# A fused two-layer transformer kernel on one core: first norms and weights reordered, two key batches closed in three steps, filler products on TensorE

## The reference

```python
x = L0_attn_hidden_states                       # (2, 1024, 256)
xn = _layernorm(x)
x = x + _L0_attn_ref(xn, ...) + _L0_ffn_ref(xn, ...)
xn = _layernorm(x)
x = x + _L1_attn_ref(xn, ...) + _L1_ffn_ref(xn, ...)

def _L0_attn_ref(h, ...):     # linear attention, 16 heads of 16
    qp, kp = elu(q) + 1.0, elu(k) + 1.0
    kv = einsum('bhsd,bhse->bhde', kp, v)
    z = einsum('bhsd,bhd->bhs', qp, kp.sum(axis=2))[..., None]
    return (einsum('bhsd,bhde->bhse', qp, kv) / (z + EPS)) @ o_w.T + o_b

def _L0_ffn_ref(x, ...):      # weights cut to -1, 0, 1 times mean(|W|)
    return (silu(x @ wu.T) * (x @ wg.T)) @ wd.T

def _L1_attn_ref(x, ...):     # rotary positions, softmax(q k / 4) v
def _L1_ffn_ref(x, ...):      # Hadamard transforms around a silu-gated FFN
```

## Time and profile before

| | before |
|---|---|
| median of 3 runs | 740.97 us (739.71, 740.97, 741.88) |
| the profiled execution's own time | 741.94 us |
| its span, first to last instruction | 740.0 us |
| mean granted TensorE clock | 0.975 |
| PE busy | 696.3 us, 94% |
| DVE / ACT / POOL busy | 71% / 59% / 40% |

### The profile page before, as it was taken

How to read it: one execution, slowest core, us unless ns; L and a number is a source line. 1 busy time by engine, 2 the same in 40 slices (tenths; PEclk the granted TensorE clock), 3 DMA queues, 4 the chain that set the end, 5 groups by cost and what they waited for, 6 DMA issues and landing times.

```text
span 740.0 us, 10943 instructions
## 1 busy us (share of the span) xinstructions
PE 696.3 (94%) x4186; PEld 437.3 (59%) x4186; DVE 524.2 (71%) x856; ACT 438.6 (59%) x600; POOL 295.8 (40%) x269
## 2 busy tenths in 40 slices
PE   3788899989999899999999998999999999999998
PEld 3576798977787778677677673333333333333345
DVE  4877866555578366678788878888897288888315
ACT  2454334446544532432432336999998899999883
POOL 1118846347657843542543431122224223333410
PEclk7799999999999999999999998999999999999999
DMA  6127101003024553423110112244444244423321
GB/s 260 57 77 279 58 0 58 1 2 115 0 86 152 182 166 98 140 90 115 57 58 2 57 58 76 80 144 151 139 138 149 93 147 141 157 90 94 102 81 58
DMA packets 25847, 74.13 MB, mean 100 GB/s; under 512 B 4620, under 2 KB 5996, under 8 KB 24964
## 3 DMA queue, kind: packets, MB, share of 16 engines
q1 hardware_dynamic: 21268, 65.37, 26.4%
q0 software_dynamic: 3808, 7.60, 3.5%
q10 hardware_dynamic: 720, 0.48, 0.2%
HBM read 54.54 MB, written 23.06 MB: 105 GB/s over the span
## 4 chain that ended last, share of the span: by engine, by line
PE 62%; POOL 2%; DVE 2%; ACT 1%; issue 1%; DMA 1%; SPq 0%; DVEq 0%; POOLq 0%; ACTq 0%
PE PS L1029 17%; PE PS L767 12%; PE PS L1015 12%; PE PS L773 9%; PE PS L998 6%; PE PS L988 5%; DVE mx L1329 1%; POOL sg L1642 1%; ACT P L1541 1%; DMA scr_k<-spl 1%; POOL rot L1663 1%; POOL rot L1662 1%; PE PS L1004 0%; ACT spl L1523 0%; ACT us L1506 0%
## 5 line engine op out<-in xcount | busy, mean ns | idle before, releaser
L1541 ACT ACTIVATE P<-PS 128x1024 f32<-128x1024 f32 x256 | 249.2, 1023 | 31.9 <-PE PS L1015 31.6
L1336 DVE TENSOR_REDUCE mx<-PS 128x1 f32<-128x512 f32 x300 | 189.2, 683 | 34.3 <-PE PS L998 32.7
L1329 DVE TENSOR_REDUCE mx<-PS 128x2 f32<-128x1024 f32 x106 | 124.8, 1221 | 37.4 <-PE PS L988 37.0
L1029 PE MATMUL PS<-P,VV 128*32 128x512 f32 x1024 | 137.6, 609 | 0.1
L1633 POOL TENSOR_TENSOR hl<-sg,hh 128x512 fp32r<-128x512 f32 x64 | 85.2, 1332 | 116.7 <-ACT hh L1511 67.4
L1015 PEld LDWEIGHTS PS<-QS,KS 64*128 64x128 f32 x512 | 48.9, 185 | 124.3 <-ACT P L1541 111.2
L1015 PE MATMUL PS<-QS,KS 64*128 64x512 f32 x512 | 117.7, 459 | 2.3 <-DVE mx L1329 1.8
L998 PE MATMUL PS<-KM,QM 64*128 64x512 f32 x300 | 82.0, 401 | 0.0
L1497 ACT ACTIVATE sg<-PS,cols 128x512 f32<-128x512 f32 x32 | 22.0, 688 | 82.1 <-PE PS L767 82.1
L1642 POOL TENSOR_TENSOR sg<-sg,us 128x512 f32<-128x512 f32 x32 | 42.1, 1316 | 37.5 <-ACT us L1506 37.5
L767 PE MATMUL PS<-XH,UGH 128*128 128x512 f32 x128 | 54.2, 423 | 1.6 <-ACT sg L1497 0.8
(11 more groups left out here) (211 smaller groups left out, 1346.6 us busy)
## 6 DMA issues: line engine op xcount, KB each, us to landing
QM<-scr_q SPq DMA_DIRECT2D x16, 512.0 KB, 4.4
KM<-scr_k SPq DMA_DIRECT2D x16, 512.0 KB, 5.3
QS<-scr_q SPq DMA_DIRECT2D x16, 512.0 KB, 4.3
KS<-scr_k SPq DMA_DIRECT2D x16, 512.0 KB, 5.2
scr_q<-spl SPq DMA_DIRECT2D x24, 256.0 KB, 3.3
scr_k<-spl SPq DMA_DIRECT2D x24, 256.0 KB, 3.4
scr_o<-OE POOLq DMA_DIRECT2D x14, 256.0 KB, 2.7
stg<-in_tern SPq DMA_DIRECT2D x3, 1024.0 KB, 4.8
```

The costliest lines, as they stand in the source:

```text
L1029: i = e.matmul(PS[32 * c:32 * c + 32, 7, :], v_head(8 * b + kt, 2 * j + c // 2), P[s % 4][:, chunk(c // 2 + 2 * (c % 2))], start=(kt == 0) ...
L1329: e.tensor_reduce(mx[p % 2][:, :, qt, half], PS[:, b:b + 2, :], AX.X, ALU.max).then_inc(q["mx"], 2)
L1336: e.tensor_reduce(mx[p % 2][:, h, qt, half:half + 1], bank[b], AX.X, ALU.max).then_inc(q["mx"], 1)
L1541: e.activation(P[s % 4][:, half * 1024:(half + 1) * 1024], PS[:, b:b + 2, :].rearrange("p b n -> p (b n)"), ACT.Exp).then_inc(q["ex"], 1)
```

## The change

- The first pieces are reordered: norm 1 ahead of turn 0, stats 2 and turn 0 ahead of the first weights; stats 3, norm 3 and turn 3 later among the first key tiles; the four POOL bias additions one to three pieces earlier.
- `FIRST` goes from 12 to 11 and `RATE0` from 0.8 to 0.83, so the FFN of layer 0 begins one side step earlier and the side work is advanced a little faster.
- `kv_end` yields after the last `kv_sum`, and again after the last three `kv_out`, so FFN pieces come between them. The two `kv_end` together have four steps more than before.
- Filler products (`busy`): 20 instead of 8 at `start`; 6 and 6 into bank 7 ahead of the first key tile, the second six after W0H; 5 into bank 2 ahead of `att_n(3)`; 4 and 2 ahead of the first and second score step. Their results are never read.

```diff
--- before.py
+++ after.py
@@ -17,10 +17,10 @@
 EARLY, MOST = 106, 3
 
 PROJECT = (56, 112, 120)
-FIRST = 12
+FIRST = 11
 
 WHOLE = 2
-RATE0 = 0.8
+RATE0 = 0.83
 
 COST = {"v": 0.7, "ln_turn": 1.0, **{n + a: 0.7 for n in ("gate", "up", "down") for a in ("", "_a")}}
 APART = 2.06
@@ -57,6 +57,9 @@
         self.i = (self.i + 1) % len(self.slots)
         return self.slots[self.i]
 
+    def peek(self):
+        return self.slots[(self.i + 1) % len(self.slots)]
+
     def pair(self):
         if self.i % 2 == 0:
             self.next()
@@ -114,8 +117,10 @@
 
     def kv_end(b):
         put("kv_sum", 8 * b + 7)
+        yield
         for tt in range(8 * b + 5, 8 * b + 8):
             put("kv_out", tt)
+        yield
         put("kv_sums", b)
         yield
 
@@ -124,6 +129,8 @@
         yield
 
     def att_n(tt):
+        if tt == 3:
+            put("busy", 5, 2)
         put("att_n", tt, ps.next())
         yield
 
@@ -279,30 +286,27 @@
     put("start")
     put("load_wa0")
     ln0 = [layernorm(c, pf) for c in range(NCH)]
-    for i in (0, 1, 0):
+    for i in (0, 1, 0, 1, 0, 2):
         next(ln0[i])
     put("w0h")
-    for i in (0, 1):
-        next(ln0[i])
     put("w0l")
-    for i in (1, 2):
-        next(ln0[i])
+    next(ln0[1])
+    put("busy", 6, 7)
+    put("busy", 6, 7, "w0h", 1)
+    next(tn)
     put("signs")
     sd0 = side0()
     next(sd0)
     next(ln0[2])
-    next(tn)
     next(sd0)
-    next(ln0[2])
-    next(ln0[3])
     for n in range(FIRST):
         if n < 10:
             next(tn)
         next(sd0)
-        if n < 2:
-            next(ln0[3])
-        if n > 7:
-            put("bias", 0, n - 8)
+        if n < 4:
+            next(ln0[2 if n == 0 else 3])
+        if n > 6:
+            put("bias", 0, n - 7)
     put("half")
     put("load_down")
     put("load_ob1")
@@ -408,6 +412,8 @@
                         later(PROJECT[g] + i, "project", g, i // 2, i % 2)
             elif piece[0] in ("times", "high", "low", "join"):
                 put(*piece)
+        if s < 2:
+            put("busy", 4 - 2 * s, mxr.peek())
         if live:
             put("scores", s, 0, st.pair())
             for _ in range(kept):
@@ -785,7 +791,14 @@
 
             def start():
                 e.wait_ge(q["init"], 1)
-                sums(bank[7][:, 0:128], [(ONES[:, :], ONES[:, :])] * 8)
+                sums(bank[7][:, 0:128], [(ONES[:, :], ONES[:, :])] * 20)
+
+            def busy(n, b, *after):
+
+                claim(b)
+                if after:
+                    e.wait_ge(q[after[0]], after[1])
+                sums(bank[b][:, 0:128], [(ONES[:, :], ONES[:, :])] * n)
 
             def ln_turn(n, *banks):
                 for b in banks:
@@ -1083,7 +1096,7 @@
                             o = two_tiles(bank[acc[2 * cc + i]], r, ((LH[:, ts], WLH[:, cc, :]), (LH[:, ts], WLL[:, cc, :]), (LL[:, ts], WLH[:, cc, :])), False, True)
                         o.then_inc(q["lp"], 1)
 
-            parts = {f.__name__: f for f in (start, ln_turn, tern_scale, kv_in, kv_out, q0, att_n, att_t, att_b, add_vb, prep_down, prep_ug,
+            parts = {f.__name__: f for f in (start, busy, ln_turn, tern_scale, kv_in, kv_out, q0, att_n, att_t, att_b, add_vb, prep_down, prep_ug,
                                              gate_a, gate, up_a, up, down_a, down, ffn_end, qk, v, max_half, max_rows, scores, values, project, last)}
             parts["max"] = max_tile
             for name, *args in order:
```

## The result

| | before | after |
|---|---|---|
| median of 4 runs each | 740.91 us (739.71 to 741.88) | **747.41 us** (746.14 to 747.69) |
| ratio, 95% interval | | **1.0086** [1.0074, 1.0098] |
| profiled execution, its span | 741.94, 740.0 | 747.69, 745.6 |

The forecast was 737.8, faster; the kernel became 6.5 us slower, and lies outside the range. In the diff's lines those of the helpers moved by 6 (L767 is L773), the ones of DVE, ACT and POOL by 13 (L1419 is L1432).

What follows compares the result with a forecast made beforehand. PE, busy 94% of the span, bounds the kernel; gains come only from its idle or half-clock time. 741.94 - 1.1 (first part) - 3.0 (first scores) = 737.8 us, range 733.0 to 742.5.

Steps and rivals of the forecast that it cites:

- The middle: 80 to 445 us: the same pieces shift by a place or two; 0 gained, with 1.5 us either way.
- The start: First norms, weights and key tiles: first key product at 18.8 us, 1.1 us earlier; first two tiles 2.5 us less.
- What eats it: First FFN blocks: PE waits of 2.8, 2.3 and 5.6 us reduce the 3.8 us lead to 1.1.
- that of 5.6 us: First FFN chunk: PE idle 5.6 us ahead of the first `down`, until DVE's second cut of TD at 70.9.
- my 1.1: Net gain of the first part: 2.6 - 3.2 + 2.85 - 1.1 = 1.1 us.
- my 3.2 us of deferred work: Tile 9, `att_n(2)` and `att_b(0)`, done before the first `down` in the kernel before, now come later: -3.2 us.
- the lead stays: Rival: DVE fills its waits, PE waits about 2 us at the first `down`; first part +5, total 733.9; chance 0.22.
- The fillers ahead of attention result 3: Five fillers ahead of `att_n(3)`, 10 records at 0.113: cost 1.1 us, since PE is no longer idle there.
- The first scores: Fillers there are hidden and keep the clock from falling at 448.2: 3.0 us gained, or 0 if it falls.
- The slower rival: TD's cuts come no earlier, PE's idle at the first `down` brings half clock: first part -4.7, total 743.6; chance 0.12.
- The base of the sum: The sum starts from the profiled execution, 741.94 us; the median of the runs shown was 740.97.
- my 0.8 us: If GpSimd and DVE exclude each other, `kv_sum(3)` beside a bias addition stands 0.8 us, total 738.6; nothing was added.

Runs made afterwards that it cites:

- the start alone: Kernel before with the new order of norms and weights and the start fillers; FIRST, RATE0 and kv_end as before, no other fillers: 735.47 us (0.9915).
- the fastest one: Kernel before with the changed start (norms, weights, start fillers) and the fillers at the first scores, the rest as before: 733.94 us (0.9888).
- both rows: Changed kernel with norm 7 ahead of the split of tile (1, 0), and that tile's join ahead of layer 0's last FFN end: 740.34 us (1.0001).
- the raised tail: Changed kernel with 0.08 more side steps per FFN step from step 72 of layer 0's FFN on: 743.02 us (1.0027).

## Why the prediction was wrong

- **The middle.** "I take 0, with 1.5 us either way" is the step that failed. The kernel lost 9.3 us between 223 and 325 us, more than the 6.5 us by which it became slower. I had read the order at the start, at the first FFN block and at the scores, not at the place where the two ends of a shifted list meet. "FIRST, RATE0 and kv_end add no work" was true and no answer: they move work. The steps could have been counted: 1 + 4 fewer, 2.9 more. The earlier trace rows end at 77 us; no row of mine stood beyond it until the scores. The reading that PE's waits over 0.25 us lie almost all in the first 80 us was wrong as well: 12 of 29 do, with 25.0 of 39.5 us, and four with 5.6 us stood between 205 and 295 us.
- **The start** was right in kind and too small. W0L ended at 16.9 for 17.5, the first key product was 1.6 us earlier than I had it, and the clock rose at 15.3 instead of 18.1. First zk 18.98 (forecast 20.3), first tanh 52.50 (54.2), 5.5 us ahead of before and not 3.8.
- **What eats it.** The waits are at their places, 1.95 and 1.96 us for 2.8 and 2.3, but that of 5.6 us is 1.8: the first step of TD took 1.76 us, not 2.6, and DVE filled its gaps. Of the 5.5 us at 60 some 2 are left at 83, counted at equal work, against my 1.1: the size was nearly right, but not for my reason. Of my 3.2 us of deferred work 2.5 still stood out at 83. The wait of 5.6 us did not come; two low-clock stretches (56.3 to 63.1 and 69.9 to 73.3 us, above) took its place. PE was busy for 9.4 us in them at half speed, which by my estimate cost 4.7. The kernel with start and score fillers, whose order there is before's, runs at full clock in the first of them:

```profile
56.30:63.10 6.80, 5.74 (x27) 4.09 (x26) 5.54 (x10) 2.53 (x5) 6.80 (x4) 1.00 0.98 312
```

  It has one low stretch there, 65.6 to 69.1, and keeps its 5.2 us whole. The rival "the lead stays" held for the start alone, not for the whole change.
- **The fillers ahead of attention result 3**: I took -1.1; the run can't tell it from nothing.
- **The first scores**: the clock held, as forecast, for 1.2 to 1.7 us instead of 3.0. I took ACT's idle time of the earlier trace rows as gained whole. Some of it stays (0.28 and 0.42 below), and in the changed kernel without fillers the low stretch was only 3.4 us long, not 6.8:

```profile
453.12 2.09 ACT L1554 ACTIVATE P<-PS 128x1024 f32<-128x1024 f32 x2 [5.63 <-PE PS L1028]
455.49 2.85 ACT L1554 ACTIVATE P<-PS 128x1024 f32<-128x1024 f32 x3 [0.28 <-PE PS L1028]
458.76 1.94 ACT L1554 ACTIVATE P<-PS 128x1024 f32<-128x1024 f32 x2 [0.42 <-PE PS L1028]
```

- **The slower rival** (743.6) had the right side. Its wait of 7 us at the first `down` did not come; its stretch at half clock did, behind two waits of 1.95 us, but at 83 us the kernel was still some 2 us ahead. A slower result was priced only in the first 80 us, and the time was lost elsewhere.
- **The base of the sum.** It started from the profiled execution, 1.0 us above the median, so its own terms (4.1 us) and the 3.1 us under the median do not agree. This decides nothing here.

What stays open: of the 13.5 us between the whole change and its best part, 9.0 are shown to be the order from step 72 on; of its rows only norm 7 (4.8 us) was shown to matter by itself. The 4.5 in front of it are bound to FIRST, RATE0, the steps of `kv_end`, the earlier bias additions and the five fillers together, not to one of them.

## What to carry to other kernels

When two streams of work are woven by a rate, a change of a few steps at one end shows up at the other; look where the streams meet, not only where the edit is. Keep an edit that gains by itself apart from the rate that goes with it: here start and score fillers on the old weave run in **733.9 us**, 7.5 under the kernel before, while the whole change is 6.5 over it. In an in-order list, put what is ready ahead of what waits: one row (norm 7 ahead of a split) was worth 4.8 us in the changed kernel, where the split waited for 7.14 us, and nothing in the fastest one.

When two traces of reordered work are compared by one repeated operation, check first that both have done the same other work by then. A lead can be work that is still to come.

## What the runs showed of the hardware

- **A DVE instruction waited for POOL's.** I added nothing for a bias addition beside `kv_sum`, which takes 0.41 us alone. After, on POOL and then on DVE:

```profile
37.74 2.36 POOL L1601 TENSOR_TENSOR X<-X,OB 128x1024 f32<-128x1024 f32 x1
...
71.87 4.60 POOL L1607 TENSOR_TENSOR stg<-stg,WSD 128x2048 f32<-128x2048 f32 x1
```

```profile
38.73 1.66 DVE L1239 SCALAR_TENSOR_TENSOR zk<-zk,ek 128x256 f32<-128x256 f32 x1
...
72.84 3.91 DVE L1239 SCALAR_TENSOR_TENSOR zk<-zk,ek 128x256 f32<-128x256 f32 x1
```

  Both end some 0.3 us behind POOL's instruction (40.39 against 40.10, 76.75 against 76.47), whenever they began. The Trainium skill (SBUF — State Buffer, on the shared port pair) says so: a DVE instruction with two SBUF inputs waits for the whole of a GpSimd instruction that reads SBUF and began first. The trace agrees, and my 0.8 us from that page was too low beside the 1.25 measured. The split of (1, 0) shows it too: 3.05 us beside POOL, 1.29 when it ran alone. As the path, it is a small part here: the stalls of all 16 `kv_sum` are 6.5 us after and 5.0 before.
- **Low-clock stretches wander with the order.** Between 150 and 300 us, before and after, each came at a single wait of PE of 1.3 to 3.6 us with busy work around it, but not every such wait has one (none at 148.6 and 158.4 after, waits of 1.82 and 1.30). A product of 512 columns takes 0.43 us in one and 0.23 outside. The same kernel with a row moved has them elsewhere (222.0, 242.4 and 266.3 us with norm 7 earlier, none from 229.7 to 741 with both rows). One that comes or goes can hide or double what an edit gives.
- **The start's clock varied between profiled executions.** With the same start as after, where the clock is low from 11.9 to 15.3 us, it stayed high until 34 us with RATE0 0.85 and until 41 with norm 7 earlier; the eight transposes of turn 1 took 1.09 us there and 1.97 after.
- **Transposes and the clock** stay open. Behind 1.97 us of transposes from 12.25 on, the clock rose 1.3 us after the fillers of 14.01 began; in the fastest kernel, with the same transposes from 12.36 on, 3.8 us after those of 14.12. The Trainium skill (TensorE: Matmul & The Clock Gate, Part 4) has transposes not count as busy. These two runs do not decide it.
- **Spread.** Some versions varied from run to run by up to 1% (738.94 to 746.09 in ten runs of the one with the raised tail) where all runs of the kernel before lay between 737.2 and 742.5. Four runs do not tell 1 to 2 us between two versions apart.
